# Expert tiles gathered by token number in place of rows scattered to DRAM, in a Mamba, cross-attention and MoE layer

## The reference, cut to what matters

```python
logits = x @ Wg + bg                              # (4, 1024, 8)
top2_vals, top2_idx = top_k(logits, 2)
scores = softmax(top2_vals)
h = gelu(x @ W1[e] + b1[e])                       # hidden 1024
y = h @ W2[e] + b2[e]
out = sum over the two chosen e of score * y
return _layer_norm(x + out, gamma, beta)          # one more norm follows, around x plus this
```

## Time and profile before

| | |
|---|---|
| three runs | 3590.22, 3602.61, 3610.32 us, median 3602.61 |
| the profiled execution | 3597.66 us, its span 3596.2 us |
| busy | PE 2781.3 us (77%), DVE 2321.5 (65%), ACT 1926.9 (54%), POOL 1726.3 (48%) |
| mean granted TensorE clock | 0.914 of 2.4 GHz |
| chain that ended last | PE 48%, DVE 24%, issue 13%, ACT 11%, DMA 2% |
| written to and read from HBM | 42.34 and 126.75 MB |

### The profile page before, as it was taken

The page is one execution under the profiler, slowest core; times in us unless marked ns, Lnnn a source line. Parts: engine busy times, 40 slices in busy tenths (PEclk is TensorE's granted clock), DMA queues, the critical chain, the costliest instruction groups (busy, mean ns, idle before and its releaser), DMA issues.

```text
span 3596.2 us, 45601 instructions
## 1 busy us (share of the span) xinstructions
PE 2781.3 (77%) x15274; PEld 2047.5 (57%) x15275; DVE 2321.5 (65%) x3190; ACT 1926.9 (54%) x3239; POOL 1726.3 (48%) x1807
## 2 busy tenths in 40 slices
PE   3787788788887995787888878888994299999920
PEld 2566666666675653566666656665653166666610
DVE  3888988988882444988988888872442033333348
ACT  4877887887871335886787887771331011212100
POOL 1777667777781002777777776771102501000052
PEclk8999899999998997999899999998995599999965
DMA  6111111111111100111111111111003212111022
GB/s 224 30 36 33 32 34 33 33 36 39 40 43 53 36 1 24 36 34 33 32 35 33 36 33 41 40 39 41 24 1 116 81 63 92 63 61 63 32 75 74
DMA packets 100973, 171.52 MB, mean 48 GB/s; under 512 B 14514, under 2 KB 52658, under 8 KB 100786
## 3 DMA queue, kind: packets, MB, share of 16 engines
q1 hardware_dynamic: 82066, 119.38, 10.4%
q0 software_dynamic: 15392, 47.99, 3.6%
q10 hardware_dynamic: 3328, 1.76, 0.2%
HBM read 126.75 MB, written 42.34 MB: 47 GB/s over the span
## 4 chain that ended last, share of the span: by engine, by line
PE 48%; DVE 24%; issue 13%; ACT 11%; DMA 2%; POOL 1%; SPq 1%; another core or an unknown queue 0%; DVEq 0%; ACTq 0%; POOLq 0%; PEld 0%
PE psD L1061 16%; DVE arena L1585 10%; PE psD L1383 7%; PE psD L1157 5%; PE psA L1177 4%; ACT arena L909 3%; DVE arena L1533 3%; ACT arena L899 2%; PE psA L1061 2%; PE psD L1260 2%; PE psA L1235 2%; PE psA L1167 2%; PE psD L1281 2%; PE psA L1374 1%; PE psD L1126 1%
## 5 line engine op out<-in xcount | busy, mean ns | idle before, releaser
L708 POOL TENSOR_TENSOR arena<-arena 128x512 f32<-128x512 f32 x1024 | 1149.7, 1150 | 16.8 <-DVE arena L1585 6.2
L1157 PE MATMUL psD<-ident,arena 128*128 128x128 f32 x4096 | 683.0, 292 | 343.7 <-DVE arena L1585 317.2
L1157 PEld LDWEIGHTS psD<-ident,arena 128*128 128x128 f32 x4096 | 478.8, 147 | 597.9 <-DVE arena L1585 399.1
L909 ACT ACTIVATE arena<-arena,negA 128x512 f32<-128x512 f32 x1024 | 715.8, 711 | 36.8 <-DVE arena L1585 36.4
L1585 DVE TENSOR_TENSOR_SCAN arena<-arena,carry,psD 128x512 f32<-128x512 f32 x512 | 640.1, 1268 | 108.3 <-PE psA L1177 97.3
L1585 DVE TENSOR_TENSOR_SCAN arena<-arena,psD 128x512 f32<-128x512 f32 x512 | 611.7, 1208 | 116.7 <-PE psA L1177 99.1
L1177 PE MATMUL psA<-ident,arena 128*128 128x128 f32 x4096 | 644.2, 283 | 0.0
L899 ACT ACTIVATE arena<-arena,bc 128x512 f32<-128x512 f32 x768 | 545.7, 711 | 116.2 <-PE psD L1157 115.7
L1177 PEld LDWEIGHTS psA<-ident,arena 128*128 128x128 f32 x4096 | 508.6, 148 | 2.1 <-issue 2.1
L692 POOL TENSOR_SCALAR arena<-arena,bc 128x512 f32<-128x512 f32 x256 | 183.7, 718 | 500.4 <-PE psD L1157 462.5
L1061 PE MATMUL psD<-arena 128*128 128x512 f32 (+4 forms) x776 | 336.3, 569 | 46.0 <-POOL strip L652 31.1
(11 more groups left out here) (214 smaller groups left out, 3709.5 us busy)
## 6 DMA issues: line engine op xcount, KB each, us to landing
arena<-c_dram SPq DMA_DIRECT2D x256, 256.0 KB, 3.1
arena<-in_W POOLq DMA_DIRECT2D x16, 1024.0 KB, 7.6
xs_dram<-arena SPq DMA_DIRECT2D x20, 512.0 KB, 7.5
arena<-xs_dram SPq DMA_DIRECT2D x71, 128.0 KB
ys_dram<-arena POOLq DMA_DIRECT2D x70, 128.0 KB, 2.0
arena<-in_x SPq DMA_DIRECT2D x8, 1024.0 KB, 7.2
o_dram<-arena SPq DMA_DIRECT2D x32, 128.0 KB, 1.7
arena<-o_dram SPq DMA_DIRECT2D x4, 1024.0 KB, 5.6
```

The source lines that it names most:

```text
L708: pool.tensor_tensor(h_ring[:, c % H_SLOTS, :], h_ring[:, c % H_SLOTS, :], c_rows[:, v % C_SLOTS, :], ALU.mult).then_inc(c_weighed, 1)
L909: act.activation(da_ring[:, c % DA_SLOTS, :], dt[:, i % 2, f, :], ACT.Exp, scale=negA[:, f, n:n + 1]).then_inc(da_ready, 1)
L1157: mm = pe.transpose(psD[:, c % FILL_BANKS, j * P:(j + 1) * P], g[:, (c // KI) % 2, j, c % KI * P:(c % KI + 1) * P], ident[:, :])
```

## The change

Nothing is scattered any more. After `slot`, VectorE splits each row number into tile (`slot_hi`) and row within the tile (`slot_lo`), and compares both with a row of column numbers: `one_lo` is a 128x128 one-hot matrix for each of 64 columns of tokens and choices, `one_hi` a 128x81 one, multiplied by the token number. The sum of 64 products on TensorE is the 128x81 table of token numbers, `token_of`; a row that no token has gets token 0. POOL gathers tile after tile from `x2_dram` into `ys`, 81 indirect DMAs, and counts `xs_sorted` up three gathers behind. SP copies a tile from `ys` to `tile_in`. For this all four batches are stored to `x2_dram`. `xs_dram` and its zeros are gone. Batches 0 and 1 are fetched back while batches 2 and 3 are in memory and xattn; behind the last norm only batch 2 is. The order of the batches in the router is 0, 1, 3, 2.

```diff
-        batch_order = [0, B - 1] + list(range(1, B - 1))
+        batch_order = [0, 1, 3, 2]
...
-            rows = xs_dram.rearrange("(p r) d -> p (r d)", p=P)
-            for c in range(-(-(TILES + 1) // 4)):
-                lo, hi = c * 4 * D, min((c + 1) * 4 * D, (TILES + 1) * D)
-                sp.dma_start(rows[:, lo:hi], zeros[:, 0:hi - lo]).then_inc(xs_zeroed, 16)
...
                     if b + 2 < B:
                         sp.dma_start(xin[:, u, :, :], x[b + 2].rearrange("(t p) d -> p t d", p=P)).then_inc(x_loaded[u], 16)
+                    else:
+                        sp.wait_ge(x2_stored, 16 * (u + 2))
+                        sp.dma_start(x2[:, u * TT:(u + 1) * TT, :], x2_dram[u * TT:(u + 1) * TT].rearrange("t p d -> p t d"))\
+                          .then_inc(x2_first, 16)
...
-            sp.dma_start(x2[:, 0:TT, :], x2_dram[0:TT].rearrange("t p d -> p t d")).then_inc(x2_first, 16)
-            sp.dma_start(x2[:, TT:NT - TT, :], x2_dram[TT:NT - TT].rearrange("t p d -> p t d")).then_inc(x2_middle, 16)
-            sp.wait_ge(xs_sorted, 16 * 2 * NT)
+            sp.dma_start(x2[:, 2 * TT:3 * TT, :], x2_dram[2 * TT:3 * TT].rearrange("t p d -> p t d")).then_inc(x2_middle, 16)
+            keep_x2(B - 1)
             sp.wait_ge(routed, 1)
-            sp.dma_start(tile_in, xs_dram[0:P, :]).then_inc(xs_loaded, 16)
+            sp.wait_ge(xs_sorted, 1)
+            sp.dma_start(tile_in, ys[:, 0, :]).then_inc(xs_loaded, 16)
...
-                sp.dma_start(tile_in, xs_dram[bass.ds(i * P + P, P), :]).then_inc(xs_loaded, 16)
+                sp.wait_ge(xs_sorted, i + 2)
+                sp.dma_start(tile_in, ys[:, bass.ds(i + 1, 1), :].rearrange("p o d -> p (o d)")).then_inc(xs_loaded, 16)
...
-            pool.wait_ge(x2_first, 16)
-            pool.wait_ge(x2_middle, 16)
-            pool.wait_ge(routed, 1)
-            for r in range(2):
-                for t in range(NT):
-                    pool.indirect_dma_start(xs_dram, bass.IndirectOffsetOnAxis(slot[:, r, t:t + 1], 0), x2[:, t, :], None)\
-                        .then_inc(xs_sorted, 16)
+            pool.wait_ge(x2_stored, 16 * (B + 1))
+            pool.wait_ge(dve_drained, END_D + 7 + RING)
+            for i in range(TILES + 4):
+                if i < TILES + 1:
+                    pool.indirect_dma_start(ys[:, i, :], None, x2_rows, bass.IndirectOffsetOnAxis(token_of[:, i:i + 1], 0))\
+                        .then_inc(token_in[i % 4], 16)
+                if i >= 3:
+                    pool.wait_ge(token_in[(i - 3) % 4], 16 * ((i - 3) // 4 + 1))
+                    pool.sem_inc(xs_sorted, 1)
...
+            for n in range(2 * NT):
+                if n % 16 == 0:
+                    pe.wait_ge(one_hot, (n // 16 + 1) * 17)
+                mm = pe.matmul(psD[:, (END_D + 6) % RING, 0:TILES + 1], one_lo[:, n, :], one_hi[:, n, :],
+                               start=n == 0, stop=n == 2 * NT - 1)
...
             dve.tensor_copy(slot[:, :, :], rest[:, 5:7, :]).then_inc(routed, 1)
+            link(dve.tensor_scalar(scaled, place_of, 1.0 / P, -(P - 1) / (2.0 * P), ALU.mult, ALU.add))
+            link(dve.tensor_scalar(scaled, scaled, ROUNDER, None, ALU.add))
+            link(dve.tensor_scalar(slot_hi, scaled, ROUNDER, None, ALU.subtract))
+            link(dve.tensor_scalar(slot_lo, slot_hi, float(P), None, ALU.mult))
+            link(dve.tensor_tensor(slot_lo, place_of, slot_lo, ALU.subtract))
+            for c in range(2 * NT // 16):
+                dve.tensor_tensor(one_lo[:, 16 * c:16 * c + 16, :], column.unsqueeze(1).broadcast_to([P, 16, P]),
+                                  slot_lo[:, 16 * c:16 * c + 16].unsqueeze(2).broadcast_to([P, 16, P]), ALU.is_equal)\
+                   .then_inc(one_hot, 1)
+                for n in range(16 * c, 16 * c + 16):
+                    dve.tensor_scalar(one_hi[:, n, :], column[:, 0:TILES + 1], slot_hi[:, n:n + 1], token[:, n % NT:n % NT + 1],
+                                      ALU.is_equal, ALU.mult).then_inc(one_hot, 1)
+            dve.wait_ge(dve_full, END_D + 7)
+            dve.tensor_copy(token_of, psD[:, (END_D + 6) % RING, 0:TILES + 1]).then_inc(dve_drained, 1)
```

More of the change, by code:

```diff
@@ L96, in decoder_layer @@
     STEPS = B * T // P
+    ROUNDER = 1.5 * 2.0 ** 23
     with ExitStack() as ctx:
@@ L109, in decoder_layer @@
         o2_dram = nc.dram_tensor("o2_dram", (2, TT, P, D), F32, kind="Internal").ap()
-        x2_dram = nc.dram_tensor("x2_dram", (NT - TT, P, D), F32, kind="Internal").ap()
-        xs_dram = nc.dram_tensor("xs_dram", ((TILES + 1) * P, D), F32, kind="Internal").ap()
+        x2_dram = nc.dram_tensor("x2_dram", (NT, P, D), F32, kind="Internal").ap()
         ys_dram = nc.dram_tensor("ys_dram", (TILES * P, D), F32, kind="Internal").ap()
@@ L229, in decoder_layer @@
         x2 = carve(NT * D).rearrange("p (t d) -> p t d", d=D)
-        ys = carve(TILES * D).rearrange("p (t d) -> p t d", d=D)
+        ys = carve((TILES + 1) * D).rearrange("p (t d) -> p t d", d=D)
         ys_flat = ys.rearrange("p t d -> p (t d)")
@@ L240, in decoder_layer @@
         tileT = carve(KD * P).rearrange("p (k t) -> p k t", k=KD)
+        token_of = carve(TILES + 1).bitcast(U32)
+        one_lo = ys_flat[:, 0:2 * NT * P].rearrange("p (n c) -> p n c", c=P)
+        one_hi = ys_flat[:, 2 * NT * P:2 * NT * (P + TILES + 1)].rearrange("p (n c) -> p n c", c=TILES + 1)
         small = in_w_sb[:, :, :].rearrange("p k f -> p (k f)")
@@ L257, in decoder_layer @@
         steps_i = read_w_sb[:, 1, :].bitcast(I32).rearrange("p (e j) -> p e j", e=E)
+        slot_hi, slot_lo, scaled = (top_words.rearrange("p t e -> p (t e)")[:, 0:2 * NT] for top_words in (top, topf, sel1))
+        column_i, column = wq_sb[:, 0, 0:P].bitcast(I32), wq_sb[:, 1, 0:P]
+        token_i, token = wo_sb[:, 0, 0:NT].bitcast(I32), wo_sb[:, 1, 0:NT]
         count = read_w_sb[:, 0, 0:E]
@@ L342, in decoder_layer @@
         xs_zeroed = sem("xs_zeroed")
+        token_in = [sem(f"token_in{q}") for q in range(4)]
         xs_sorted = sem("xs_sorted")
+        one_hot = sem("one_hot")
         xs_loaded = sem("xs_loaded")
@@ L509, in decoder_layer @@
         LOADED = 16 * len(loads)
-        ZEROED = 16 * (-(-(TILES + 1) // 4) + (TILES - FEWEST) // 4)
+        ZEROED = 16 * ((TILES - FEWEST) // 4)
         def load_expert(engine, e, r):
@@ L741, in _ @@
             pool.iota(steps_i, pattern=[[0, E], [P, STEPS]], base=0, channel_multiplier=0).then_inc(steps_ready, 1)
+            pool.iota(column_i, pattern=[[1, P]], base=0, channel_multiplier=0).then_inc(steps_ready, 1)
+            pool.iota(token_i, pattern=[[P, NT]], base=0, channel_multiplier=1).then_inc(steps_ready, 1)
             for e in range(2):
                 load_expert(pool, e, e)
-            pool.wait_ge(x2_first, 16)
-            pool.wait_ge(x2_middle, 16)
-            pool.wait_ge(routed, 1)
-            for r in range(2):
-                for t in range(NT):
-                    pool.indirect_dma_start(xs_dram, bass.IndirectOffsetOnAxis(slot[:, r, t:t + 1], 0), x2[:, t, :], None)\
-                        .then_inc(xs_sorted, 16)
+            pool.wait_ge(x2_stored, 16 * (B + 1))
+            pool.wait_ge(dve_drained, END_D + 7 + RING)
+            x2_rows = x2_dram.rearrange("t p d -> (t p) d")
+            for i in range(TILES + 4):
[5 more added lines that the diff above has]
+                    pool.sem_inc(xs_sorted, 1)
             def keep_results(e):
@@ L1331, in _ @@
             pe.wait_ge(ln_done, B * 2 * TT)
[L1332 to L1338, removed]
+            pe.wait_ge(x2_first, 32)
+            for j, q in enumerate(batch_order):
+                if q == 2:
+                    pe.wait_ge(x2_middle, 16)
                 turn_x2(q)
-            for q in range(1, B - 1):
-                logits(q)
+                if j >= 1:
+                    logits(batch_order[j - 1])
+            logits(batch_order[B - 1])
             pe.wait_ge(route_step, SEL_STEP)
@@ L1347, in _ @@
                           start=True, stop=True).then_inc(dve_full, 1)
+            claim_d(END_D + 6)
+            for n in range(2 * NT):
[3 more added lines that the diff above has]
+                               start=n == 0, stop=n == 2 * NT - 1)
+            mm.then_inc(dve_full, 1)
             def turn_tile(i):
@@ L1388, in _ @@
             pe.sem_inc(turn_full, 2)
-            pe.wait_ge(dve_drained, END_D + 6 + RING)
+            pe.wait_ge(dve_drained, END_D + 7 + RING)
             pe.wait_ge(act_drained, END_A + KD * CH + RING)
@@ L1730, in _ @@
             link(dve.tensor_tensor(rest[:, 4, :], rest[:, 1, :], rest[:, 3, :], ALU.mult))
-            dve.wait_ge(steps_ready, 1)
+            dve.wait_ge(steps_ready, 3)
             link(dve.tensor_copy(steps, steps_i))
+            link(dve.tensor_copy(column, column_i), wait=False)
+            link(dve.tensor_copy(token, token_i))
             for j, dst in enumerate((place, total)):
@@ L1757, in _ @@
```

(3 more changed lines are left out.)

## The result

| | median us | shown runs |
|---|---|---|
| before | 3602.61 | 3590.22 to 3610.32 |
| changed | 3631.76 | 3616.77 to 3633.69 |
| ratio | 1.0081 | 95% interval 1.0053 to 1.0108 |

The changed kernel is slower by 0.8 per cent, where 1.8 per cent of gain was forecast. The part of the change that leads up to the experts did most of what was said. What was lost lies right behind it, in a stretch that the prediction had costed at nothing.

The account below looks back on a forecast made before the run. No single engine was taken to bound the whole; routing by scatter was bound by the number of descriptor-writing instructions. Gains of 11.3 - 0.2 + 52.7 = 63.8 us gave 3539 us against the median, ratio 1.018, range 3521 to 3561.

Parts of the forecast that it names:

- Early fetch, gain 11.3: Router logits behind the last norm: batches 0, 1 and 3 already in SBUF, batch 2 hidden, 11.3 us gained.
- Rival 2: Router logits: batch 2 comes late beside store and weights, TensorE stands 8 us, 3547 us in all; chance 0.08.
- VectorE, 18.5 us of comparisons and tensor_scalar: Routing behind slot: four comparisons, 8.8 us, and 64 tensor_scalar at 0.151 us, 9.7 us; sum 18.5 us.
- Token numbers, 24.5 us after slot: One-hot products on TensorE: at the high clock token numbers are ready 24.5 us after slot, bounds 23.4 and 32.9.
- rival 1: Logits and one-hot products: TensorE stays at 1.2 GHz, 16.8 us less gain, 3556 us; chance 0.10.
- Gather to SP's read, 6.0 us: Start of the gathers: SP is released when gather 0 is in and gather 3 is issued, 6.0 us.
- Sum up to the first product: From the last norm to the first expert product: 11.3 - 0.2 + 52.7 = 63.8 us gained.
- "Cost 0" for what the gathers are now beside: First experts beside the other 77 gathers: tiles always there, expert 2's weights 57 us early, so cost 0.
- rivals 3 and 4: Expert loop: VectorE slows gathers, expert 2's weights 27 us late (3566 us, chance 0.04) or 99 (3638, chance 0.03).
- "The final stage is untouched": Final stage behind the expert loop: claimed unchanged, with no term in the sum.

Follow-up runs that it names:

- e1: The kernel before with only the change's batch order and early fetches of batches 0 and 1; 3577.22 against 3590.27 us, ratio 0.9968.
- e5: The changed kernel with POOL gathering one tile at a time, paced by the loop, and SP issuing stores and weights; 3519.72 us, ratio 0.9850.
- e7: The changed kernel with POOL waiting for each gather to land before issuing the next; 3681.91 us, against 3573.99 for the kernel before on its chip.

## Why the prediction was wrong

By its own steps:

- *Early fetch, gain 11.3*: right, and by its mechanism. Logits were done 31.7 us after the norm (32.0 forecast), TensorE did not wait for batch 2, and e1 measured it alone. Rival 2 did not happen.
- *VectorE, 18.5 us of comparisons and tensor_scalar*: 23.7. The comparisons took 2.2 us each as forecast, but the 64 tensor_scalar came in portions of 16 in 3.80 us, so 0.23 us each and not 0.151. That is 5.1 us more. Scaling the norm's 256-element row down to 81 elements was the error; that row has two column operands from two tiles as well, so the operands are not the difference, and whether its fixed part or its part by elements fell short was not tried. The faster estimate worked out from the Trainium skill (VectorE: DVE Perf Modes, "The perf-mode tier table"), 7.0 us for the 64, was further off still: they took 14.8.
- *Token numbers, 24.5 us after slot*: 35.1. This is rival 1's clock, here for the one-hot products only: 0.50 throughout, 128 passes in a row.

```profile
2757.72 27.56 PE L1366 MATMUL psD<-arena 128*128 128x81 f32 x128 [14.13 <-DVE arena L1794]
2785.32 0.24 DVE L1797 CAST arena<-psD 128x81 uint32<-128x81 f32 x1 [10.03 <-PE psD L1366]
```

  0.215 us a pass, and a first portion that came 1.4 us later than forecast: 2.2 us above my upper bound of 32.9. As TensorE was the pace, VectorE's 5.1 us cost only that 1.4. I had chosen the high level because TensorE reached it 4 us into an earlier stretch. That one began with transposes, after 11.8 us of idle time; this one with these thin products, after 14.1. What made the difference was not tried.
- *Gather to SP's read, 6.0 us*: 3.8. SP was released at 2789.34, before gather 3 had begun (2790.34). From there to the first product 5.5 us instead of 4.7.
- *Sum up to the first product*: 63.8 forecast, 55.1 measured. With this alone the kernel would have come out near 3548, inside the range.
- *"Cost 0" for what the gathers are now beside*: this is the step that failed, by 88.4 us. I asked of the gathers only whether they would be there in time, and whether VectorE would slow them (rivals 3 and 4). They were not slowed: 1.257 us apart, and the third expert's weights were not late. Tile i+1 was always there, as I had said; its turn came late. The harm ran the other way, from the gathers to the loop, and no rival had it. A row for it was on the page that I used: the 6.47 us that VectorE waited for a releaser without a name in the final stage, between gathers 1.25 us apart. I read that stretch for the length of the gathers, not for what stood beside them. By the kernel, line 1829 waits there for a count that VectorE alone raises (`fin_step`), and VectorE's last instruction before it had ended at 3483.88. So there it was VectorE's own release that came 6.5 us late: the effect is not one of TensorE alone.
- *"The final stage is untouched"*: 5.2 us longer. The changed kernel's VectorE waits 12.3 us there for unnamed releasers, the kernel before 10.8 us; in e5 and e7 there is no such wait, although their 64 last gathers are mostly 1.25 us apart as well: by the semaphore events each of VectorE's 276 releases there is out within 0.02 us. So a row this dense does not always delay releases, and what else it takes is not explained. The final stage also blurs e5's gain: its profile has 57.9 us less up to the first product and 16.2 us less behind the last tile, against 54 us measured beside the kernel before on its own chip, of which there is no trace.

By the Trainium skill (SBUF — State Buffer, "Who interferes with whom") the gathers and this loop should leave each other alone, and TensorE and ScalarE wait for no one at SBUF's ports. The rows agree in that no instruction of theirs got longer than its clock makes it; what was late are releases, of which the section does not speak.

## What to carry to other kernels

Before you put a row of indirect DMAs beside a stage that passes its work between engines, look whether the trace has such a row beside any hand-over, and read the waits of the others there. Here 81 of them, most 1.26 us apart, held an 8 us loop to less than two tiles in 100 us, while one for each tile was free and made the kernel 1.5 per cent faster than before. "Hidden behind other work" is a claim about both sides: ask what the hidden work does to its cover.

## What was not expected of the hardware

- Beside indirect DMAs issued by GpSimd 1.26 us apart, releases from TensorE came 12, 23 and 57 us late, in order; releases from VectorE to TensorE in the same stretch took 0.06 us. In the final stage of the kernel before, VectorE's own came up to 6.5 us late; in that of e5 and e7, at the same distance, none did. Neither 27 instead of 103 GB/s nor an otherwise empty queue changed it; 1.9 us apart on average, or plain DMAs with POOL busy for 0.81 of the time, did away with it. Which path the late releases share with the gathers, and at what distance between 1.26 and 1.9 us it begins, was not tried. Nor was a part of the profiler's own recording: where releases are late, semaphore events are missing too (228 of VectorE's 276 are there in the final stage before, all in e5's).
- The last gathers of the changed kernel, for tiles that hold no tokens and so read row 0 128 times, drove the DMA share to 0.84 at 78 GB/s, where it had been 0.34 at 104. That they all read one row is a likely cause and was not tested.

```profile
2860.00:2870.00 10.00, 0.00 (x0) 0.00 (x0) 0.00 (x0) 0.00 (x0) 7.56 (x9) 0.50 0.34 104
2880.00:2890.00 10.00, 0.00 (x0) 0.00 (x0) 0.00 (x0) 0.00 (x0) 5.50 (x7) 0.50 0.84 78
```
